# Attention probabilities a pair later, even units on ScalarE and VectorE, low check by sums

## The reference, cut to what matters

```python
q = _mxfp4_matmul(x, wq_codes, wq_scales) + bq      # w = codes * repeat(scales, 32)
k = _mxfp4_matmul(x, wk_codes, wk_scales) + bk
v = _mxfp4_matmul(x, wv_codes, wv_scales) + bv
scores = jnp.einsum('bqhd,bkhd->bhqk', q, k) / jnp.sqrt(128.)
attn = jax.nn.softmax(scores, axis=-1)
out = jnp.einsum('bhqk,bkhd->bqhd', attn, v).reshape(B, S, 16 * 128)
return _mxfp4_matmul(out, wo_codes, wo_scales) + bo
...
x = x + _layernorm(attention(_layernorm(x)))
x = x + _layernorm(experts(_layernorm(x)))          # top 6 of 64, capacity 96, plus a shared expert
```

## Time and profile before

| | |
|---|---|
| median of 3 executions | 1334.64 us (1333.19 to 1335.9) |
| profiled execution, span from the first to the last instruction | 1341.9 us |
| granted TensorE clock, mean | 0.983 |
| attention, from the first row maximum to the last | 32.55 to 979.3 us |
| the tail | to 1341.9 us |

### The profile page before, as it was taken

How to read it: one execution, slowest core, us unless ns; L and a number is a source line. 1 busy time by engine, 2 the same in 40 slices (tenths; PEclk the granted TensorE clock), 3 DMA queues, 4 the chain that set the end, 5 groups by cost and what they waited for, 6 DMA issues and landing times.

```text
span 1341.9 us, 25318 instructions
## 1 busy us (share of the span) xinstructions
PE 1207.5 (90%) x7852; PEld 844.1 (63%) x7852; DVE 860.6 (64%) x2297; ACT 825.8 (62%) x2128; POOL 931.0 (69%) x1130
## 2 busy tenths in 40 slices
PE   4889999999999999989999999998958799989995
PEld 1556666666666666657666666665635378777973
DVE  5898567687678768767876876777676233222226
ACT  3666678768777776877777677777745133223413
POOL 4896456678878877986888798688764624444557
PEclk9899999999999999999999999999989899999998
DMA  7774987755555354354534545434445359898676
GB/s 257 173 191 94 228 211 150 163 102 120 122 99 118 73 116 94 73 108 82 93 68 98 97 69 94 79 70 81 81 100 165 112 166 259 226 234 213 131 211 227
DMA packets 364678, 182.68 MB, mean 136 GB/s; under 512 B 287440, under 2 KB 343222, under 8 KB 364544
## 3 DMA queue, kind: packets, MB, share of 16 engines
q1 hardware_dynamic: 344960, 166.18, 52.5%
q0 software_dynamic: 16416, 11.70, 4.9%
q10 hardware_dynamic: 3168, 3.15, 0.7%
HBM read 75.32 MB, written 64.69 MB: 104 GB/s over the span
## 4 chain that ended last, share of the span: by engine, by line
PE 39%; DVE 18%; DMA 14%; POOL 13%; issue 7%; ACT 5%; another core or an unknown queue 2%; SPq 1%; ACTq 0%; POOLq 0%; DVEq 0%
DMA PT<-PH 8%; PE bank L1066 7%; PE bank L1037 6%; PE bank L1081 6%; DMA Y<-W,wix 5%; POOL PH L972 4%; POOL P L967 4%; PE bank L1052 4%; PE bank L1098 3%; PE bank L1206 3%; DVE nm L1455 3%; PE bank L1219 2%; POOL BUF L716 2%; PE bank L1130 2%
## 5 line engine op out<-in xcount | busy, mean ns | idle before, releaser
L967 POOL TENSOR_SCALAR P<-P,rr 128x256 f32<-128x256 f32 x512 | 249.2, 498 | 141.2 <-DVE rr L1451 132.2
L1308 ACT ACTIVATE P<-bank,nm 128x256 f32<-128x256 f32 x512 | 237.2, 468 | 149.2 <-DVE nm L1455 140.9
L972 POOL TENSOR_TENSOR PH<-P,PH 128x512 f16<-128x512 f32 x256 | 296.2, 1171 | 20.1 <-ACT PH L1317 19.1
L1037 PE MATMUL bank<-RB,W 128*128 128x512 f16 x1076 | 257.9, 382 | 7.2 <-ACT Sx L645 4.2
L716 POOL DMA_INDIRECT BUF<-RT,ix x192 | 197.8, 1030 | 91.3 <-issue 42.2
L1066 PE MATMUL bank<-RB 128*128 128x256 f32 x1024 | 245.7, 383 | 2.7 <-issue 2.5
L1081 PE MATMUL bank<-PT,RB 128*128 128x256 f16 x1536 | 197.2, 273 | 36.1 <-DMA PT<-PH 32.1
L1455 DVE TENSOR_REDUCE nm<-bank 128x2 f32<-128x512 f32 x256 | 174.3, 682 | 51.1 <-PE bank L1066 50.5
L1081 PEld LDWEIGHTS bank<-PT,RB 128*128 128x128 f16 x1536 | 145.1, 98 | 95.9 <-DMA PT<-PH 50.5
L1066 PEld LDWEIGHTS bank<-RB 128*128 128x128 f32 x1024 | 185.7, 191 | 26.2 <-issue 3.8
L1317 ACT ACTIVATE PH<-P 128x512 f16<-128x512 f32 x256 | 161.4, 630 | 55.7 <-POOL P L967 38.9
(11 more groups left out here) (207 smaller groups left out, 1600.0 us busy)
## 6 DMA issues: line engine op xcount, KB each, us to landing
RB<-in_ewT SPq DMA_DIRECT2D x24, 352.0 KB
BUF<-zrow SPq DMA_DIRECT2D x4, 1926.0 KB, 8.4
W<-BUF SPq DMA_DIRECT2D x64, 120.4 KB
HT<-in_ewT SPq DMA_DIRECT2D x18, 352.0 KB
HT<-in_wc SPq DMA_DIRECT2D x24, 256.0 KB, 4.3
HT<-in_ws SPq DMA_DIRECT2D x24, 256.0 KB, 4.7
Y<-zrow SPq DMA_DIRECT2D x10, 512.0 KB, 3.5
RB<-in_ewd SPq DMA_DIRECT2D x24, 176.0 KB
```

The lines of the kernel that those rows point to most:

```text
L967: r = eng.tensor_scalar(p, p, rr[:, w % 4, t:t + 1], SP_, ALU.mult, ALU.mult)
L972: eng.tensor_tensor(PH[:, w % 2, 1, :], P[:, w % 2, :], PH[:, w % 2, 0, :], ALU.subtract).then_inc(s["pl"], 1)
L1037: r = eng.matmul(bk_[:, :], W[:, m, a, c * 2048 + h * 128:c * 2048 + (h + 1) * 128], XT[:, bp % 2, b, c, :], start=(k == 0), stop=(k == n ...
L1308: r = eng.activation(P[:, u % 2, t * 256:(t + 1) * 256], bS[u % 2][:, t * 256:(t + 1) * 256], ACT.Exp, bias=nm0[:, u % 4, t:t + 1], accum_ ...
```

## The change

It has three parts.

- The product with V and WO come later: PV at lags 4 and 3 (before: 2 and 1), WO at lag 6 in the even and the odd slot (before: 4 and 3 in the even one), O's parts at lags 5 and 6. In PE's order PV now stands before V, and WO behind it. PH and PT get a third buffer each (`PHB`, `PTB`) in the space of `SSf`; the shared expert's down weights are therefore loaded at slot 232 into XN. `END` becomes 263.
- Even units leave GpSimd: ScalarE copies the exponentials times a column `r64` (the reciprocal times 64, made by `scale` on VectorE) to the high part, in two halves of 256, and VectorE multiplies and subtracts for the low part, in two halves. Odd units stay as they were, `norm` and the low part on GpSimd. The semaphore `pl` becomes `pld` and `plp`.
- The low check moves to ScalarE: one `Abs` of 512 with its sum for each of the 32 blocks, at the slots `CHECK_AT`. The flag is "some sum is above zero".

The slots in `PLACE` are all given anew: those of the jobs after attention start at slot 6 of the next group (before: 3) and end at 37 on VectorE (before: 35) and 62 on GpSimd (before: 55); they are left out here.

```diff
-W_AT = (0, 0, 1, 2, 2, 3, 4, 5, 5, 6, 7, 7, 8, 9, 10, 10, 11, 12, 12, 13, 14, 15, 15, 16)
+W_AT = (0, 0, 1, 2, 2, 3, 5, 5, 6, 7, 8, 9, 9, 10, 11, 13, 13, 13, 13, 14, 16, 16, 16, 17)
...
+CHECK_AT = (1, 1, 1, 1, 2, 2, 2, 2, 3, 3, 4, 5, 5, 6, 8, 8, 9, 10, 11, 12, 12, 13, 14, 16, 16, 16, 16, 17, 19, 19, 19,
+ 19)
...
+NPT = 3
-ORDER = {
-    "pe": ([("S", 0), ("S", -1), ("Q", -2), ("K", -2), ("WO", 4), ("WO", 3), ("V", -6), ("PV", 2), ("PV", 1),
-                ("bg", 0)],
-           [("bg", 0)]),
-    "act": ([("exp", 0), ("bg", 0), ("exp", -1)],
-           [("Q", -1), ("P", 1), ("V", -5), ("P", 0), ("O", 3), ("bg", 0)]),
-    "dve": ([("max", 0), ("O", 4), ("max", -1), ("bg", 0), ("recip", 0), ("bg", 0), ("bg", 0)],
-           [("bg", 0), ("recip", 0), ("K", -1), ("bg", 0), ("V", -5), ("bg", 0)]),
-    "pool": ([("bg", 0)],
-           [("norm", 1), ("norm", 0), ("P", 1), ("P", 0), ("bg", 0)]),
-    "sp": ([("bg", 0), ("T", 1)],
-           [("bg", 0), ("T", 1)]),
-}
+ORDER = {'pe': ([('S', 0), ('S', -1), ('Q', -2), ('K', -2), ('PV', 4), ('PV', 3), ('V', -6), ('WO', 6), ('bg', 0)],
+        [('bg', 0), ('WO', 6)]),
+ 'act': ([('bg', 0), ('exp', 0), ('exp', -1), ('bg', 0), ('Q', -2)],
+         [('P', 1), ('V', -5), ('P', 0), ('bg', 0), ('O', 5), ('bg', 0)]),
+ 'dve': ([('max', 0), ('O', 6), ('max', -1), ('bg', 0), ('recip', 0), ('scale', 0), ('bg', 0)],
+         [('recip', 0), ('K', -1), ('bg', 0), ('P', 1), ('bg', 0), ('V', -5)]),
+ 'pool': ([('bg', 0)], [('norm', 0), ('bg', 0), ('lo', 0), ('bg', 0)]),
+ 'sp': ([('bg', 0), ('T', 1)], [('bg', 0), ('T', 1)])}
...
-PE_AT = (17, 19, 23, 31)
-STORE_AT = (18, 20)
+PE_AT = (19, 20, 25, 33)
+STORE_AT = (18, 18)
-KEEP_AT = (22, 24)
+KEEP_AT = (22, 34)
...
+        SSh = SSf[:, :].bitcast(F16)
+        PHB = [PH[:, 0, :, :], PH[:, 1, :, :], SSh[:, 0:1024].rearrange("p (l n) -> p l n", l=2)]
+        PTB = [PT[:, 0, :, :, :, :], PT[:, 1, :, :, :, :],
+               SSh[:, 1024:2048].rearrange("p (l t c q) -> p l t c q", l=2, t=2, c=2)]
...
+        unused = sb("unused", [128, 512], F16)
...
+        r64 = sb("r64", [128, 4, 2])
...
-        lowbits = C1[:, :, :].rearrange("p t e -> p (t e)").bitcast(U32)
+        lowsum = C1[:, 0, 0:32]
...
-        sdf = SSf[:, 0:768].rearrange("p (j n) -> p j n", j=3)
+        sdf = XN[:, 0:3, :]
...
-        names = ("c0 cg cd gt S e r pn ph pl pv oh ol wo q ql k kl v vh vl xc po wm wh wl "
+        names = ("c0 cg cd gt S e r rs pn ph pld plp pv oh ol wo q ql k kl v vh vl xc po wm wh wl "
...
-        s_pt = [sem(f"s_pt{i}") for i in range(2)]
+        s_pt = [sem(f"s_pt{i}") for i in range(NPT)]
...
+            def check(eng):
...
-                if n == 0:
-                    eng.tensor_scalar(lowbits, lo.bitcast(U32), NOSIGN, None, ALU.bitwise_and).then_inc(s["lf"], 1)
-                else:
+                if n:
...
-                    eng.scalar_tensor_tensor(out=lowbits, in0=lo.bitcast(U32), scalar=NOSIGN, in1=lowbits,
-                                             op0=ALU.bitwise_and, op1=ALU.bitwise_or).then_inc(s["lf"], 1)
+                eng.activation(unused[:, :], lo, ACT.Abs, accum_out=lowsum[:, n:n + 1]).then_inc(s["lf"], 1)
...
+            plan["act"].setdefault(CHECK_AT[n], []).append(check)
...
         def flag_jobs():
             def rows(eng):
...
-                return eng.tensor_reduce(low1, lowbits, AX, ALU.max)
+                return eng.tensor_reduce(low1, lowsum, AX, ALU.max)
...
-            return LC.step("dve", FLAG_AT + 3, lambda e: e.tensor_scalar(low3, low2, 1.0, None, ALU.min))
+            return LC.step("dve", FLAG_AT + 3, lambda e: e.tensor_scalar(low3, low2, 0.0, None, ALU.is_gt))
...
             def turn_p(w):
-                eng.wait_ge(s["pl"], w + 1)
-                if w >= 2:
-                    eng.wait_ge(s["pv"], w - 1)
-                eng.dma_start_transpose(PT[:, w % 2, :, :, :, :].rearrange("p l t c q -> p (l t c) q"),
-                                        PH[:, w % 2, :, :].rearrange("p l n -> p (l n)")).then_inc(s_pt[w % 2], 16)
+                eng.wait_ge(s["pld" if w % 2 == 0 else "plp"], w // 2 + 1)
+                if w >= NPT:
+                    eng.wait_ge(s["pv"], w - NPT + 1)
+                eng.dma_start_transpose(PTB[w % NPT].rearrange("p l t c q -> p (l t c) q"),
+                                        PHB[w % NPT].rearrange("p l n -> p (l n)")).then_inc(s_pt[w % NPT], 16)
...
+                if slot == 232:
+                    eng.wait_ge(s["xc"], XC.n)
...
-            eng.wait_ge(s["pl"], NU)
+            eng.wait_ge(s["pld"], NI)
+            eng.wait_ge(s["plp"], NI)
...
-            for k in range(2):
-                eng.wait_ge(s_pt[k], 16 * NI)
+            for k in range(NPT):
+                eng.wait_ge(s_pt[k], 16 * len(range(k, NU, NPT)))
...
-            def p_low(w):
+            def p_low_plain(w):
...
-                eng.tensor_tensor(PH[:, w % 2, 1, :], P[:, w % 2, :], PH[:, w % 2, 0, :], ALU.subtract
-                                  ).then_inc(s["pl"], 1)
+                eng.tensor_tensor(PHB[w % NPT][:, 1, :], P[:, w % 2, :], PHB[w % NPT][:, 0, :], ALU.subtract
+                                  ).then_inc(s["plp"], 1)
...
-                slot_work("pool", u, {"norm": norm, "P": p_low, "bg": lambda *a: run_plan("pool", eng, *a),
+                slot_work("pool", u, {"norm": norm, "lo": p_low_plain, "bg": lambda *a: run_plan("pool", eng, *a),
...
-                eng.wait_ge(s_pt[u % 2], 16 * (u // 2 + 1))
+                eng.wait_ge(s_pt[u % NPT], 16 * (u // NPT + 1))
...
-                                       PT[:, u % 2, b, :, kc, :], start=(k == 0), stop=(k == 5))
+                                       PTB[u % NPT][:, b, :, kc, :], start=(k == 0), stop=(k == 5))
...
             def exp(u):
...
-                    eng.wait_ge(s["pl"], u - 1)
+                    eng.wait_ge(s["pld" if u % 2 == 0 else "plp"], u // 2)
...
             def p_high(w):
-                eng.wait_ge(s["pn"], w + 1)
-                if w >= 2:
-                    eng.wait_ge(s_pt[w % 2], 16 * (w // 2))
-                eng.activation(PH[:, w % 2, 0, :], P[:, w % 2, :], ACT.Copy).then_inc(s["ph"], 1)
+                if w >= NPT:
+                    eng.wait_ge(s_pt[w % NPT], 16 * (w // NPT))
+                hi = PHB[w % NPT][:, 0, :]
+                if w % 2 == 0:
+                    eng.wait_ge(s["rs"], w // 2 + 1)
+                    for t in range(2):
+                        r = eng.activation(hi[:, t * 256:(t + 1) * 256], P[:, 0, t * 256:(t + 1) * 256],
+                                           ACT.Copy, scale=r64[:, w % 4, t:t + 1])
+                else:
+                    eng.wait_ge(s["pn"], w // 2 + 1)
+                    r = eng.activation(hi, P[:, 1, :], ACT.Copy)
+                r.then_inc(s["ph"], 1)
...
+            def scale(w):
+                eng.wait_ge(s["r"], w + 1)
+                eng.tensor_scalar(r64[:, w % 4, :], rr[:, w % 4, :], SP_, None, ALU.mult).then_inc(s["rs"], 1)
+            def p_low(w):
+                eng.wait_ge(s["rs"], w // 2 + 1)
+                eng.wait_ge(s["ph"], w + 1)
+                for t in range(2):
+                    n = slice(t * 256, (t + 1) * 256)
+                    r = eng.scalar_tensor_tensor(out=PHB[w % NPT][:, 1, n], in0=P[:, 0, n],
+                                                 scalar=r64[:, w % 4, t:t + 1], in1=PHB[w % NPT][:, 0, n],
+                                                 op0=ALU.mult, op1=ALU.subtract)
+                r.then_inc(s["pld"], 1)
             def row_max(u):
...
-            work = {"recip": recip, "max": row_max, "O": o_low,
+            work = {"recip": recip, "scale": scale, "P": p_low, "max": row_max, "O": o_low,
...
             def shared_low(n):
```

26 lines of the change are left out of this document (9 added, 17 removed), and 13 rows, old and new, of the table PLACE.

## The result

The changed kernel takes 1285.38 us (median of 4, 1284.55 to 1292.43) where the kernel before takes 1335.27 (median of 4, 1333.19 to 1338.43): ratio 0.964, interval 0.961 to 0.967. The prediction was 1303, in a range of 1282 to 1336. So the sign and the range hold, and the gain is 50 us where 32 were forecast. The profiled execution has a span of 1283.9 us.

The account below looks back on a forecast made before the run. PE was taken to bound the kernel, with waits for transposed blocks and VectorE's O above its floor. Terms -4 - 3 - 26.5 + 1.5 = -32 us, from the median 1334.64, gave 1303, range 1282 to 1336.

Parts of the forecast that it names:

- Stage: -34.5 + 8 = -26.5: The 108 steady pairs: 34.5 us of PE's block waits go, VectorE's added load costs 8, so 26.5 us less.
- +8: Steady stage: VectorE's added work for even units delays K, O and V for PE by 8 us, bounds -18 to +97.
- The floor: Steady stage without PE's waits for blocks and VectorE's low part of O: 731 us, 6.77 a pair.
- rival (b): Steady stage: PE's waits for blocks and for O both vanish, saving about 65 us: 1270 to 1280; chance 0.09.
- holds gone, load harmless: Steady stage, lower bound of the effect of VectorE's work on PE: its waits for O vanish, -18 us.
- (a): Steady stage: VectorE at 90% turns 20 to 25 of 34.5 us into other waits; saving 10 to 18, 1320; chance 0.16.
- within what is counted: New slots of router, weight and store steps: they move by a few slots, with no term of their own.
- Pairs 0 to 8, -4: First nine pairs: the low check leaves VectorE, ScalarE gains 20 us; 86.7 becomes about 83 us, bounds 80 and 92.
- Of the 4.6 us without work the deeper buffers take 3 away: Stage 119 to 173 us, beside the clearing of the buckets: PE's idle 4.6 us shrink by 3.
- 1 to 2 us once: Flag step at slot 19: VectorE waits for four checks on ScalarE, 1 to 2 us, counted within pairs 0 to 8.
- The end, +1.5: After the last scores: two early shared-expert products of 2.6 us each stand ahead of WO; +1.5 us, bounds 0 and 5.
- Rival (c): Steady stage: a two-input VectorE step per pair is held 1.17 us by GpSimd; VectorE becomes the bound, 1352; chance 0.10.

Follow-up runs that it names:

- without the delay: Changed kernel with PV back at lags 2 and 1 and WO at 4 and 3, three buffers kept: 1338.24 us, ratio 1.008 to the kernel before.
- before with part 2 alone: Kernel before with only the even units' high and low parts moved to ScalarE and VectorE: 1337.08 us, ratio 1.003.
- without part 2: Changed kernel with even units' multiplications and low part back on GpSimd, later PV and three buffers kept: 1321.61 us, ratio 0.995.
- The old places in the kernel after: Changed kernel with the slots of the kernel before, router steps from before slot 6 put at slot 6: 1322.52 us, ratio 0.993.
- mixing the checks: Changed kernel with even weight blocks checked by VectorE's bits, odd ones by ScalarE's sums: 1299.56 us, ratio 0.962 to the kernel before.

## Why the prediction was right, and where its sum was off

**What was right.** Faster, with the time in the range; the waits for blocks gone (3 us were left to them, 0 are there); O as what is late next, at the product with V; GpSimd's work down by 615.6/108 - 388.1/108 = 2.11 us a pair (2.17); ScalarE at 607.0/108 = 5.62 (5.73); ScalarE the busiest helper of pairs 0 to 8 with 72.1 of 78.9 us. The function table is not loaded between the checks. There are four loads in the whole span, as before, and the first is the one of the earlier trace rows; its row in the groups of ScalarE:

```profile
L533 ACT ACT_TABLE_LOAD x1 | 1.3, 1283 | 0.8 <-PEq L1612 0.8
```

This agrees with the Trainium skill (ScalarE: Activation LUTs, section Table sets: the hidden batching unit), which puts abs in every set.

**The term that was mis-sized: "Stage: -34.5 + 8 = -26.5".** It measured -51.4. Its first half held (-37.5 for blocks). Its second half had the wrong sign. The waits for O were given +8 and changed from 18.1 to 14.7 us, by -3.4 (by -5.8 if 2.4 us of "issue" at WO are counted, which also start right behind O). The rest lies in waits for which the sum had no term. Those of the earlier trace rows's view that are gone are, in us: 5.7 at the product with V and 1.7 at the scores without a releaser, 4.6 for ScalarE's normed rows, 3.0 for VectorE's transposed rows, 2.4 and 1.8 at WO, together 19.2. All the waits that the view names went from 83.2 to 25.1 us, by 58.1; the stage got back 51.4 of that.

**The floor was nearly reached, but not as rival (b) says.** (b), "both waits vanish", had 0.09. One of them vanished and the other mostly stayed, while others that the floor of 6.77 had left in went instead. That 6.81 comes so near 6.77 is therefore partly luck.

**VectorE's load** was the reason for the +8. I put it at 6.3 us a pair and 90%; it was 5.78 and 85%. I had added the new work to the old work *at its old durations*, holds included. The holds went, 45.7 us in six Newton lines of which three are shown above, and that paid for more than a third of the 118.2.

The row was there: line 405 with 161 ns as its median and 2,623 as its longest. The bounds in the prediction had even priced it (-18, "holds gone, load harmless"), and I took +8 for a reason of load alone. How much of the stage's gain the holds are worth is not shown: without the delay they are nearly gone as well, and nothing is won.

Two sums of the rivals don't come out. (a) gives back 20 to 25 us of a gain of 32, which leaves 7 to 12 and not 10 to 18; and the second 3 in (b)'s sum has no row.

**Both causes of the holds count.** GpSimd's two-input work per pair halves with part 2, but that isn't enough: before with part 2 alone has the same GpSimd work as after, and its subtractions are still 100 ns longer, its Newton step 285 ns. Nor are the places alone: without part 2 and with the new places, L400 has a mean of 214 ns (before 420, after 160; 180 to 900 us). The old places in the kernel after give 218. The two together give 160, with the delay or without it (159).

**Why the parts are not a sum.** PE waits for the last of several things. Without the delay that is the transpose behind VectorE's low part, whoever does the rest (38.6 us). With it, it is O: 35.0 us of waits without part 2, 26.4 with the old places, 14.7 with all. On the 108 pairs the delay and the new places without part 2 give 18 us, the delay and part 2 with the old places give 18 too, part 2 and the new places without the delay give none, and all three give 51. So two of the three give at most 18 of the 51 without the third. The delay with neither of the others was not run, and the new places are made for the whole of the change, so the runs with a part undone may be slower than that part's absence must be. Rival (a) described well a kernel without the delay.

**The placements: "within what is counted".** This step failed. They are worth 34 us with the other parts in place, less what putting the first router steps together at slot 6 costs in that run, which was not tried apart. A step that is "moved by a few slots" next to a VectorE at 85% decides whose turn O comes behind.

**Pairs 0 to 8, -4 against -7.8.** The 25 OR steps went, as said, and ScalarE did not become the bound at 80: it has 72.1. 5.4 of the gain is part 3's by its undoing. Of ScalarE's work, 4 of 26 high parts of weights (2.6 us) left the stage by the new `W_AT`, and 28 of the 32 checks fell into it. The check's price, 0.628 us with a read of 0.194 behind it, is the upper bound (0.83), not the 0.63 that I took. Groups of ScalarE in pairs 0 to 8:

```profile
L543 ACT ACTIVATE unused<-W 128x512 f16<-128x512 f16 x28 | 17.6, 628 | 2.6 <-DVE W L537 1.8
...
L543 ACT ACTIVATION_READ_ACCUMULATOR unused<-W 128x1 f32 x28 | 5.4, 194 | 0.0
```

**"Of the 4.6 us without work the deeper buffers take 3 away": +6.2 instead.** I read 119 to 173 by the share of PE and gave the buffers credit for stalls whose causes I had not looked up. There are two. The flag's wait was foreseen ("1 to 2 us once") but put into the stage before, and measured 3.5. The clearing of the buckets holds SP's queue itself: the transposes' issues take about three times as long there, ScalarE waits for a buffer, and O comes late. The third buffer did not cover that. Spreading the clearing takes 5.0 of the 6.2 away, mixing the checks 3.2, and both at once bring the stage to 52.6, below the 54.0 of before.

**The end, +1.5 against +4.2.** I said that "the chain from exponential to sums is the same" and counted only the two shared products. But both products stood there before too (983.36 and 989.94 us in the timeline of PE). What is new is a pair's PV and WO more behind the last scores, 1.3 + 0.9 us (four WO against three), and the waits for O that go with them, 1.0 to 1.6 us each. The size lies within the bounds (0 to 5), its reason was the wrong one.

**Rival (c), held subtractions at the pace of GpSimd,** did not come: 0.50 us each. The rule of the Trainium skill that it stood on (GPSIMD Engine Reference, section Specifications) is not refuted. The trace agrees with it in pairs 0 to 8, where GpSimd still has its two-input weight products of 1.33 us (L529): there the new subtractions take 0.55 to 0.61 us, against 0.50 in the steady stage. Of the two lines that the prediction puts under that rule, line 398 has a single input in SBUF; that it runs in a two-port mode no run shows. By the same rule I could have priced the old conflicts that the change removes.

## What to carry to other kernels

When work leaves an engine, reprice the neighbour's old instructions too: a short operation with a maximum many times its median is a hold, and it goes when its partner goes. When a wait for a block is to be removed, list what the consumer would wait for next, and expect that parts which each give little alone may give much together; test them in pairs before dropping one. Where a view of waits says "issue", look in the timeline at what ended just before: here, at the product with V, it was VectorE's O in nearly every case. A large clear on the queue that also issues small critical transfers should be cut up and spread, even where its total stays the same.

## What the runs showed of the hardware that I had not expected

- A DMA transpose's issue on SP takes 1.23 us alone and 3.1 to 4.7 us beside transfers of 1,926 KB that fill the 16 engines (share 1.05 to 1.23 in stretches of 5 us), and one took 9.74 us from the start of its issue to its landing. With parts of 963 KB the issues took 1.23 to 3.05 us, by the timeline of SP's queue, and PE did not stop.
- The three VectorE operations of 4 columns shown above lasted 160 to 171 ns on average beside half the two-input work of GpSimd in other places, and 307 to 798 beside all of it.
- ScalarE's copy of 256 from SBUF scaled by a column on 128 partitions, to float16, takes 512 ns; the 470 of the earlier trace rows reads PSUM, on 96 partitions, to float32.
